# Moving three pieces of work around the first self-attention units of a decoder layer's next batch

## The reference

```python
x = x + attn(layernorm(x), wq, wk, wv, wo)
x = x + cross(layernorm(x), ctx_512, Wq, Wkv_expand, Wout)
x = x + ffn(layernorm(x), w_gate, w_up, w_down)
```

## Time and profile before

| | us |
|---|---|
| median of three runs | 424.14 (423.71 to 425.94) |
| the profiled execution, its time | 424.8 |
| the profiled execution, first to last instruction (span) | 423.0 |
| PE busy | 398.2 |
| DVE busy | 286.3 |
| ACT busy | 206.1 |
| POOL busy | 160.3 |

### The profile page before, as it was taken

The page is one execution under the profiler, slowest core; times in us unless marked ns, Lnnn a source line. Parts: engine busy times, 40 slices in busy tenths (PEclk is TensorE's granted clock), DMA queues, the critical chain, the costliest instruction groups (busy, mean ns, idle before and its releaser), DMA issues.

```text
span 423.0 us, 8030 instructions
## 1 busy us (share of the span) xinstructions
PE 398.2 (94%) x2981; PEld 320.0 (76%) x2982; DVE 286.3 (68%) x610; ACT 206.1 (49%) x531; POOL 160.3 (38%) x160
## 2 busy tenths in 40 slices
PE   8998999899998899999999899999999898988996
PEld 8667778667697777777798777877789676756795
DVE  5977931779768971688858992678857992346263
ACT  1373731587335731487444642287444452188330
POOL 4552790388311420377510430167620340057000
PEclk9998999999999999999999999999999999999999
DMA  7975431312001200242001300242000400230000
GB/s 218 355 288 146 123 104 37 114 26 70 3 7 67 84 2 25 77 124 71 0 8 51 102 0 2 99 108 62 2 2 2 149 2 2 82 95 0 2 2 25
DMA packets 33447, 28.90 MB, mean 68 GB/s; under 512 B 18689, under 2 KB 28033, under 8 KB 33153
## 3 DMA queue, kind: packets, MB, share of 16 engines
q1 hardware_dynamic: 33408, 28.40, 21.4%
HBM read 19.21 MB, written 5.24 MB: 58 GB/s over the span
## 4 chain that ended last, share of the span: by engine, by line
PE 60%; DVE 18%; ACT 8%; issue 7%; POOL 4%; DMA 1%; SPq 1%; POOLq 0%; DVEq 0%; ACTq 0%
PE ps L569 13%; PE ps L442 11%; PE ps L633 7%; PE ps L512 7%; ACT prob L1178 4%; PE ps L533 3%; PE ps L451 3%; PE ps L555 3%; PE ps L649 3%; POOL prob L1071 2%; DVE mx L869 2%; DVE total L883 2%; DVE rope L841 2%; PE ps L608 2%; PE ps L494 2%
## 5 line engine op out<-in xcount | busy, mean ns | idle before, releaser
L1071 POOL TENSOR_TENSOR prob<-prob,inv 128x512 f32<-128x512 f32 x80 | 83.4, 1048 | 97.9 <-DVE inv L889 97.8
L442 PE MATMUL ps<-xnT,wqk_sb 128*128 128x256 f32 x320 | 77.9, 384 | 0.8 <-DVE rope L841 0.4
L442 PEld LDWEIGHTS ps<-xnT,wqk_sb 128*128 128x128 f32 x320 | 57.5, 190 | 12.2 <-issue 5.7
L1178 ACT ACTIVATE prob<-ps,mx 128x128 f32<-128x128 f32 (+1 forms) x128 | 53.1, 435 | 15.5 <-DVE mx L867 12.3
L1064 POOL TENSOR_TENSOR qs<-rope 128x512 f32<-128x512 f32 x32 | 40.8, 1274 | 43.4 <-DVE rope L841 40.7
L512 PE MATMUL ps<-ident_sb,prob 128*128 128x128 f32 x320 | 49.3, 278 | 7.5 <-POOL prob L1071 7.5
L1188 ACT ACTIVATE pT<-ps 128x512 f32<-128x512 f32 x80 | 48.0, 604 | 12.0 <-PE ps L512 11.7
L841 DVE TENSOR_TENSOR rope<-ps,trig_sb 64x512 f32<-64x512 f32 x74 | 50.9, 688 | 1.0
L512 PEld LDWEIGHTS ps<-ident_sb,prob 128*128 128x128 f32 x320 | 36.6, 140 | 16.4 <-POOL prob L1071 11.9
L867 DVE TENSOR_REDUCE mx<-ps 128x2 f32<-128x512 f32 (+1 forms) x48 | 32.7, 689 | 13.0 <-PE ps L494 12.4
L1050 POOL TENSOR_TENSOR rstd<-vareps,power 128x1 f32<-128x1 f32 x24 | 13.1, 550 | 73.8 <-DVE vareps L820 73.6
(11 more groups left out here) (123 smaller groups left out, 687.0 us busy)
## 6 DMA issues: line engine op xcount, KB each, us to landing
k<-kx SPq DMA_DIRECT2D x32, 128.0 KB, 2.9
q<-qx SPq DMA_DIRECT2D x32, 128.0 KB, 2.5
vb<-v_sb SPq DMA_DIRECT2D x42, 64.0 KB, 2.1
wqk_sb<-in_wqk SPq DMA_DIRECT2D x4, 512.0 KB, 7.5
work<-in_wgu SPq DMA_DIRECT2D x4, 512.0 KB, 8.8
wo_sb<-in_wo SPq DMA_DIRECT2D x1, 2048.0 KB, 14.5
vb<-v_sb SPq DMA_DIRECT2D x36, 32.0 KB, 2.2
wd_sb<-in_wd SPq DMA_DIRECT2D x1, 1024.0 KB, 5.8
```

The costliest lines, as they stand in the source:

```text
L442: mm = pe.matmul(o[:, half, :], wqk_sb[:, k, g, half, :], xnT[:, 0, k, :], start=(k == 0), stop=(k == KT - 1))
L1071: pool.tensor_tensor(p, p, inv[:, i % ND, 0:g].unsqueeze(2).broadcast_to([P, g, 512 // g]), ALU.mult).then_inc(s_norm, 1)
L1178: ins = act.activation(prob[:, i % ND, h * k:(h + 1) * k], ps[:, BANK_S + i % 2, h * k:(h + 1) * k], ACT.Exp, bias=mx[:, i % ND, h:h + 1], ...
```

## The change

Three moves, and one piece of code put into a function of its own (`first_units`):

1. `keys_rest` on DVE goes from behind the first unit's maximum to behind the first unit's sum. The same function is used ahead of batch 0, so the order changes there as well.
2. `add_out` of chunk 0's down projection goes from the end of the batch (behind the third unit's maximum) into the next batch, between `row_moments` and `normalise` of the first norm; in the last batch, where this norm is missing, it stands just ahead of `sparsify(b - 1, 1)`.
3. `magnitudes` of chunk 1 on ACT go, where there is a next batch, from behind the gates to steps i = 8 and 9 of the next batch's loop, behind `unit_out` of units 4 and 5.

```diff
+            def first_units(b, prior):
+                unit_max(b, 0)
+                for i in range(1, HEAD):
+                    unit_max(b, i)
+                    unit_sum(b, i - 1)
+                    if i == 1:
+                        keys_rest(prior)
+
             def batch(b, more):
...
                     for t in range(TT):
                         row_moments(rows[b + 1], 0, 3 * b + 2, t)
+                    if b:
+                        add_out("down", b - 1, b - 1)
                     for t in range(TT):
                         normalise(rows[b + 1], 0, 3 * b + 2, t, ("ln3", b - 1) if b else ("ln1", None))
+                elif b:
+                    add_out("down", b - 1, b - 1)
                 if b:
                     sparsify(b - 1, 1)
...
                 if more:
-                    unit_max(b + 1, 0)
-                    keys_rest(b)
-                    for i in range(1, HEAD):
-                        unit_max(b + 1, i)
-                        unit_sum(b + 1, i - 1)
+                    first_units(b + 1, b)
                 else:
                     sparsify(b, 1)
-                add_out("down", b, b)
+                    add_out("down", b, b)
...
-            unit_max(0, 0)
-            keys_rest(None)
-            for i in range(1, HEAD):
-                unit_max(0, i)
-                unit_sum(0, i - 1)
+            first_units(0, None)
...
                     if i < NQB:
                         unit_exp(b, i)
+                    elif b and i < NQB + 2:
+                        magnitudes(b - 1, 1, i - NQB)
...
                 for c in range(FC):
                     for j in range(2):
                         gate(b, c, j)
-                    for j in range(2):
-                        magnitudes(b, c, j)
+                    if c == 0 or not more:
+                        for j in range(2):
+                            magnitudes(b, c, j)
```

## The result

The changed kernel takes 421.03 us (median of 5 runs, 419.6 to 421.5); the kernel before took 423.82 us beside it. The ratio is 0.9915, with a 95% interval from 0.9893 to 0.9936: 2.8 us faster. The forecast was 419.3 us, in a range of 417.3 to 421.4. So the direction and the range hold, but the gain is only a little over half of what was worked out (2.8 against 4.86). Where the rest went can be seen in the profile.

What follows compares the result with a forecast made beforehand. PE, busy for 94% of the span, was taken as the bound, with time to regain only at its waits. 2 x 2.44 + (2.44 - 1.86) - 0.6 = 4.86 us gained gave 419.3 us, range 417.3 to 421.4.

Steps and rivals of the forecast that it cites:

- Boundary gain, 2.44 us, three times: At each of three batch boundaries DVE gains 2.44 us (1.80 idle, 0.56 addition's slot, 0.08 overlap), all passed on to PE.
- magnitudes put off, keys' rest behind the first sum: At the three boundaries, ACT's earlier exponential and key copy plus DVE's new order remove DVE's 1.80 us wait.
- Late sparsity in batches 1 and 2: Chunk 1's sparsity waits for the magnitudes; the normalised tile still comes 0.45 us before PE transposes it, costing nothing.
- Late sparsity in the last batch: With no next batch's values filling PE, the normalised tile comes 1.86 us too late, a cost paid once.
- the other case in Part 3: Last batch: if POOL had not caused the sparsity's extra 1.12 us, the loss would be 2.98 us, the time 420.4.
- The clock: Rival, 8%: PE's last-batch wait grows from 0.8 to 2.5 us, the clock falls, 1.7 us are lost: 421.0.
- The start: Ahead of batch 0, keys' rest behind the first sum makes every unit from the third 0.6 us later.
- Sum: Three boundary gains less the last batch's late tile and the start's cost: 4.86 us gained, forecast 419.3 us.
- the last batch was held: Judges a rival, 8%: later waits in the last batch take up the tile's lateness, gain 6.7 us, time 417.4.
- the table load does not wait for the subtraction: Judges a rival, 7%: ACT's table load at the boundaries waits for DVE's subtraction, gain 2.8 us, time 421.3.
- the magnitudes need no table load of their own among the exponentials: Judges a rival, 8%: ACT's put-off magnitudes need their own tables, leaving a gain of 1.3 us, time 422.9.
- the sparsity didn't become the bound: Judges a rival, 4%: magnitudes over 2.6 us later than worked out delay the sparsity in every batch; at 2.6, 426.3.

Runs made afterwards that it cites:

- the fillers: The changed kernel with four filler calls (8 matmuls) on PE in the last batch's wait before the second output projection: 419.72 us, ratio 0.9897.
- the magnitudes alone: The kernel before with the second magnitudes put off and nothing else: 425.75 us, ratio 1.0046.
- 5.: Each move made singly on the kernel before: magnitudes put off 425.75 us, keys' rest moved 420.08, addition moved 422.35, new order at the start 424.61.
- the start alone: The kernel before with the new order of the keys' rest at the start and nothing else: 424.61 us, ratio 1.0018.
- the two sets of runs: The changed kernel, unedited, measured two times: 421.03 us, ratio 0.9915, and again 420.4 us, ratio 0.9909.

## Why the prediction was right, and where it was off

- **Boundary gain, 2.44 us, three times:** measured 97.73 - 95.31 = 2.42 in the period; the sixth transpose ahead of the projection moved by 7.68 us over the three boundaries (342.40 to 334.72), of which 0.34 belong to the start, so by 2.45 each. PE could follow, as worked out.
- **Its cause** was put wrongly. The prediction began with ACT being late through the magnitudes, and treated "magnitudes put off, keys' rest behind the first sum" as one. The runs split it: 1.75 from the keys' rest, 0.6 from the addition, 0.07 from the magnitudes. With unit 1's maximum and subtraction moved in between, the first exponential has 1.32 us more, and even behind magnitudes and table load it is late by only that 0.07. The prediction's own rows held this: 227.03 + 1.28 + 0.63 = 228.94 for its end, against a first sum at 228.91.
- **Late sparsity in batches 1 and 2, free:** right (2.54 us of waiting on DVE, none on PE).
- **Late sparsity in the last batch, 1.86 us:** right as far as it went. With the fillers, at full clock, the spans are 416.4 and 416.6; before has a middle of 421.9 at full clock. 5.4 us gained against 2 x 2.44 + (2.44 - 1.86) = 5.46. The profile of the magnitudes alone, where the clock held, shows the loss by itself: its sixth transpose stands 2.70 us earlier than in before (339.70 to 342.40), the projection's third part only 0.80 (359.05 to 359.85), so 1.90 are lost. PE waits there for the bank, which the prediction named only in brackets; the normalised tile is ready at 356.04 and taken at 356.19, right behind the projection's first part. The sparsity lasts 5.22 us (343.56 to 348.78 in the changed kernel), 5.21 in the sum: its two first comparisons took 0.69 us each, and 0.96 and 1.52 in before, where POOL's normalisations ran beside them. So the 2.98 us and 420.4 of the other case in Part 3 didn't come.
- **The clock, given 8% as a rival at 421.0:** this is the term that the sum put at nothing and that failed. The step "in PE's present waits of the last batch it stayed at 1.00" took the wait of 2.44 us for a likely repeat of two waits of 0.8. None of eleven executions kept a mean clock over 0.996; the two profiled lost 2.88 and 1.25 us in the last batch. That its size (1.7 us) came near the middle of the two is luck: it was read from six microseconds at the start, whose fallen clock costs 0.82 us in the old order (see 5.).
- **The start, 0.6 us:** right only for executions whose clock has fallen there (0.59 us between the profiles of before and of the start alone), wrong for those at full clock, where it costs nothing. The forecast priced a gap that the fallen clock of the profiled execution had made. This error partly made up for the one before.
- **Sum:** 5.46 at the boundaries, the last batch's late tile already taken off; 0 for the start; less 1.3 to 2.9 for the clock. That is 2.6 to 4.2 us. Measured: 2.8 and 3.5 (the two sets of runs). So 421.03 lies in the range by the rival's mechanism, and not by the forecast's own sum, which comes out 1.7 us too fast.
- **Rivals:** the last batch was held by the late bank and tile (1.90 us), the table load does not wait for the subtraction (at 220.66 in the changed kernel, the subtraction at 224.23), the magnitudes need no table load of their own among the exponentials (the groups of instructions by line show loads ahead of the gates, L1231, and the exponentials, L1174, and one at the start, L1134, but none at the magnitudes' L1238), and the sparsity didn't become the bound outside the last batch.

## What to carry to other kernels

When a change lengthens a wait on PE, price the wait twice: once for itself and once for the clock behind it, and look whether independent matmuls can fill it. When two engines wait for each other around a short pipeline's start, first reorder the waiting engine; work put off on the other engine may be worth next to nothing and comes due later, where nothing covers it. And before a gap in a profile is priced, look at the clock in the window that ended it: a gap made by a fallen clock is there only in some executions.

## What the runs showed of the hardware

- The granted clock fell to 0.50 in a PE wait of 2.44 us in two profiled executions (for about 6.8 and 3.4 us; in both the fall came before PE had resumed) and not in a third with the same wait, 2.45 us. It fell once behind waits of 0.81 and 0.80. At the start it fell in four of the twelve profiled executions without fillers there, though all twelve have the same two waits, of 0.35 or 0.36 and of 0.42 us. The same program has it in one execution and not in another.
- DVE's norm of two tiles (two instructions behind POOL's root) took 5.55 us once, while POOL did four weight splits back to back (4.95 us) that had started 0.45 us later. In the changed kernel's profile the splits began just as far behind (56.90 against 56.44) and the norm took 1.87. Narrow windows of the timeline part the merged row: in both the first instruction takes 0.41 us and the second starts 0.06 to 0.08 us behind the first split. In the changed kernel it ends 0.15 us behind the end of this split (it lasts 1.35 us), in the other execution 0.16 us behind the end of the fourth (5.03 us). The Trainium skill ("SBUF — State Buffer", SBUF: two separate sides) says that DVE and GpSimd share a port pair as an exclusive lock: a GpSimd instruction, or a DVE instruction in a two-port mode, which `tensor_scalar` can enter, has it for the whole instruction, and the other one blocks. The ends of the second instruction fit this; no run here tries it. Why it stayed out for one split in the one execution and for four in the other isn't shown.
- In the last batch of before, DVE's first two comparisons took 0.96 and 1.52 us beside POOL's normalisations, and 0.69 each in the changed kernel, where they started behind a wait of 6.55 us and POOL had long finished its normalisations.
